# Attention and expert kernel on one core: attention-times-value groups merged in pairs, a ring of twelve exponentials, and row statistics written where they are used

## The chip, the cores and the metric

The kernel runs on one core of a Trainium2 chip. The metric is device microseconds of one execution, the median over runs. TensorE multiplies matrices and writes to the eight PSUM banks (512 fp32 columns each). VectorE, ScalarE and GpSimd do element work; SyncE and the others issue DMAs. Each engine takes its instructions in the order of its own program, and semaphores join the programs.

## The reference

Input x is 16 x 512 tokens of 256 features, so 8192 tokens. Then, cut to what matters:

```python
n = layernorm(x)
a = w[0] * mha(n @ proj_local, window=128) + w[1] * mha(n @ proj_global, window=256)
#   mha: 16 heads of 16; softmax(q @ k.T / 4 + mask) @ v; mask adds 1 above the diagonal
x1 = x + layernorm(layernorm(a) * gamma + beta)
y  = layernorm(x1)
moe = y + gate(token) * (silu(r @ w_gate[e]) * (r @ w_up[e])) @ w_down[e]
#   r = y's row; e = argmax of y @ w_router, 32 experts, at most 320 tokens of one expert, later ones dropped
out = x1 + layernorm(moe)
```

## The kernel before

**Two stages.** The attention stage goes over 32 windows of 256 tokens in a software pipeline of 36 steps. The expert stage then goes over 16 pairs of experts, from rows that the attention stage scattered to `slots_d` in HBM. In step s, window a = s is projected to q, k and v; b = s-1 has its row maxima found; c = s-2 has its exponentials and its value products; d = s-3 is projected out and normalised; f = s-4 is routed.

**Units and slots.** A window has 24 score units of 512 columns: 8 local ones (two heads of two 128-token blocks) and 16 global ones (one head). A step has 24 slots k. In each slot every engine does its part for unit k, and whatever the tables `PE_AT`, `ACT_AT` and `DVE_AT` put there: a name and the number of its slot. The order within a slot is that of the code of `step`.

- TensorE in slot k: `scores(k, c)` fills one of two banks `S2` with transposed scores (L1245, L1249 local; L1254, L1257 global), less each row's maximum, plus the mask. `tri` times the identity adds the mask. Then come the table's items, last `row_scores(k, b)` into one of two banks `S1` (L1316, L1319). Here `x2T` and `xnT` are transposes (L1351, L1357), `p0` to `p3` the q and k projections (L1288), `v0`, `v1` those of v (L1295), `lg` the router (L1371), `op0`, `op1` the output projection (L1398), `cs` the counts of the router (L1384 to L1388).
- ScalarE: `exps(k, c)` (L688) takes bank S2 to `pt`, a ring of 8 tiles of 128x512 fp32. Other items: `p` (high parts, L699), `mid` (L705), `v` (L711), and the scaling of normalised rows (L718): `norm0` the next x, `xn2` the router's input, `f1` and `z` the two inner layer norms.
- VectorE: `maximum(k, b)` (L922) reduces bank S1 to row maxima. Other items: `u` (below), `p` (L906), `f`, statistics (L849, L857), `top` and `route` (small router operations), `split` and `fold`.
- GpSimd: reciprocal roots of the variances (`inv_std`), low parts (L539), the scaling with gamma and beta, the sum `x1` (L587), and the scatter of rows (L576).

**Value products.** `values(g)` multiplies exponentials with `v_pad` for four heads into the one bank `PV`: heads go to 32-partition strips, so one matmul writes 32 partitions, and fp32 makes each matmul two instructions. A group fills 256 of the bank's 512 columns: four local groups of 16 instructions of 128 columns (L1270), four global ones of 16 of 256 columns (L1278). VectorE then turns PV in 32x32 blocks into `otok` (`unfold`, L949), after every second group takes the reciprocal of the softmax sums (L955) and multiplies (`normalise`, L963). The next `values` waits for `pv_read` of the last `unfold`. Groups 0 to 7 are at TensorE's slots 4, 6, 9, 12, 14, 18, 22 and 1 of the next step; unit u's exponential waits until the group that read its tile of the ring is through.

**Row statistics.** A token's row is 260 numbers in `xrow`: x1, mean, reciprocal deviation, gate, token number. VectorE copies mean and deviation (L1058, L1059), gate and token (L1028, L1029) into it and counts `left` down (L1035). The scatter writes the row out, and the expert stage normalises it as (x1 - mean) * rstd (L1130).

Of the kernel before, what the change touches and what calls it, by code (L numbers as in the profile page):

```python
# [8 lines left out]
def attention_moe_program(nc, T, x, pT_l, pT_g, winT_l, winT_g, woT_l, woT_g, bqk_l, bqk_g, bv_l, bv_g,  # L9
# [16 lines left out]
    GROUPS = 8  # L26
# [9 lines left out]
    MEAN, RSTD, GATE, TOKEN = D, D + 1, D + 2, D + 3  # L36
# [31 lines left out]
    with ExitStack() as ctx:  # L68
# [74 lines left out]
        okf = sb("okf", [P, 2])  # L143
        slotf = sb("slotf", [P, 2])
        far = sb("far", [P, 2])
        gate1 = sb("gate1", [P, 2])
# [3 lines left out]
        bvb = sb("bvb", [P, 4, P])  # L150
        bo = sb("bo", [P, 2, D])
# [200 lines left out]

        ACT_NORMS = (0, 1, 2, 3)
# [5 lines left out]
        def _(sp):  # L359
# [95 lines left out]
            sp.wait_ge(pv_full, GROUPS * NW)  # L455
# [25 lines left out]
        def _(pool):  # L481
# [28 lines left out]
            def inv_std(n, w):  # L510

                wait(pool, ln_var[n], w)
                if n in ACT_NORMS:
                    pool.tensor_tensor(nm[:, n, :], mv[:, n, :, 0], minus1[:, :], ALU.mult)  # L514
# [3 lines left out]
                if n in ACT_NORMS:  # L518
                    last.then_inc(rstd_made[n], 1)
                    wait(pool, rstd_made[n], w)  # L520
                    last = pool.tensor_tensor(mr[:, n, :], nm[:, n, :], rstd[:, n, :], ALU.mult)
                last.then_inc(ln_rstd[n], 1)

            def inv_std_again(w):

                wait(pool, rstd_made[3], w)
                pool.tensor_tensor(ve[:, 4, :], rstd[:, 3, :], rstd[:, 3, :], ALU.mult).then_inc(rstd_sq_made, 1)
# [14 lines left out]
            def step(s, par):  # L542
# [6 lines left out]
                if f:  # L549
                    inv_std(3, f)  # L550
                    inv_std_again(f)
# [27 lines left out]
                if d:  # L579
# [6 lines left out]
                    pool.wait_ge(xr_in[1 - par], xr_count(d))  # L586
                    pool.tensor_tensor(x1[:, 1 - par, :, :], ybuf[:, :, :], xr[:, 1 - par, :, :], ALU.add).then_inc(x1_ready, 1)  # L587
# [39 lines left out]
        def _(act):  # L627
# [51 lines left out]
            def exps(u, c):  # L679
                wait(act, s2_full, c, UNITS, u)  # L680

                if u < 8:
                    wait(act, pv_full, back(c), GROUPS, 6 + u // 4)
                elif u < 16:
                    wait(act, pv_full, c, GROUPS, (u - 8) // 2)
                else:
                    wait(act, pv_full, c, GROUPS, 4 + (u - 16) // 4)
                act.activation(pt[:, u % 8, :], S2[u % 2][:, :], ACT.Exp).then_inc(p_ready, 1)  # L688
# [18 lines left out]
            def v_out(q, b, par):  # L707
                wait(act, v_full, b, 2, q)

                wait(act, pv_full, back(b, 2), GROUPS, GROUPS - 1)  # L710
# [818 lines left out]
```

## Time and profile before

| | us |
|---|---|
| median of 3 runs (lowest, highest) | 1620.1 (1618.76, 1621.07) |
| profiled execution, its own time | 1606.68 |
| its span, first to last instruction | 1604.9 |
| mean granted TensorE clock | 0.973 |

The profiled execution is 13.4 us, 0.8%, below the median of the timed runs. The page has the busy time of every engine (PE is TensorE's matmuls, PEld its weight loads, DVE VectorE, ACT ScalarE, POOL GpSimd), and the chain that ended last. Rows of the timeline and of the chain are merged: "x16" is sixteen instructions of one line.

### The profile page before, as it was taken

Reading aid. Unit: us, or ns where it says so; the run is one execution under the profiler, and the core shown is the slowest. Engines: PE = TensorE matmul, PEld = TensorE weight load, DVE = VectorE, ACT = ScalarE, POOL = GpSimd, SP = SyncE. Lnnn points to the kernel's source line nnn. Section 1 sums busy time; section 2 is a strip of 40 time slices with the busy share of each in tenths; the row PEclk is TensorE's granted clock in tenths of the full one; section 3 lists DMA queues with packets and bytes.
Section 4 is the critical chain, followed back from the end, with each engine's and each line's share of the span. In section 5 each row is a group of like instructions: output and inputs, shape, how many; then the busy total and the mean of one; then the engine's idle time right before and its main releaser. Section 6 shows DMA issues by size and latency. Waiting matters only on the chain.

```text
span 1604.9 us, 39878 instructions
## 1 busy us (share of the span) xinstructions
PE 1496.9 (93%) x13672; PEld 1089.0 (68%) x13672; DVE 1240.0 (77%) x3785; ACT 912.3 (57%) x1919; POOL 725.1 (45%) x1097
## 2 busy tenths in 40 slices
PE   5799999999999999999999999999999945999992
PEld 3566777777777777777777777777777624777771
DVE  2677888888888888888888888888888632788874
ACT  3356667666666767666667676666666532222220
POOL 2113444444444444444444444444444341466666
PEclk9999999999999999999999999999999977999996
DMA  7997666666666766676666656656566303545540
GB/s 130 171 222 174 111 110 103 108 107 104 115 111 104 114 107 106 104 110 114 104 109 107 105 103 104 102 102 103 102 98 102 100 15 104 153 151 166 168 139 11
DMA packets 253720, 183.56 MB, mean 114 GB/s; under 512 B 29492, under 2 KB 252151, under 8 KB 253518
## 3 DMA queue, kind: packets, MB, share of 16 engines
q1 hardware_dynamic: 232414, 164.49, 55.7%
q10 hardware_dynamic: 14192, 12.79, 2.9%
q0 software_dynamic: 6912, 3.73, 0.9%
q8 instruction: 110, 1.80, 0.5%
q14 instruction: 92, 0.75, 0.2%
HBM read 55.78 MB, written 38.04 MB: 58 GB/s over the span
## 4 chain that ended last, share of the span: by engine, by line
PE 88%; DVE 2%; POOL 2%; issue 2%; DMA 2%; SPq 1%; ACT 1%; ACTq 1%; POOLq 0%; DVEq 0%
PE bank L1288 14%; PE bank L1439 9%; PE bank L1278 7%; PE bank L1319 7%; PE bank L1398 7%; PE bank L1295 7%; PE bank L1257 7%; PE bank L1270 4%; PE bank L1316 4%; PE bank L1254 3%; PE bank L1249 3%; PE bank L1245 3%; PE bank L1371 2%; PE bank L1452 2%; PE bank L1464 2%
## 5 line engine op out<-in xcount | busy, mean ns | idle before, releaser
L922 DVE TENSOR_REDUCE mx<-bank 128x2 f32<-128x512 f32 (+1 forms) x768 | 512.8, 672 | 154.8 <-PE bank L1316 96.2
L688 ACT ACTIVATE pt<-bank 128x512 f32<-128x512 f32 x768 | 449.7, 593 | 237.1 <-PE bank L1257 149.3
L1288 PE MATMUL bank<-xnT,weff 128*128 128x256 f32 x1024 | 253.8, 391 | 7.2 <-DVE rest L906 6.4
L1288 PEld LDWEIGHTS bank<-xnT,weff 128*128 128x128 f32 x1024 | 186.3, 192 | 42.1 <-issue 11.9
L1319 PE MATMUL bank<-stack 96*128 96x256 bf16 x1024 | 196.7, 273 | 5.9 <-DVE mx L922 5.7
L1257 PE MATMUL bank<-stack 100*128 100x128 bf16 x2048 | 197.9, 218 | 0.0
L539 POOL TENSOR_TENSOR parts<-rest,parts 128x512 bf16<-128x512 f32 x128 | 147.6, 1162 | 76.2 <-ACT parts L705 76.2
L554 POOL TENSOR_TENSOR obuf<-obuf,xrow 128x512 f32<-128x512 f32 x32 | 40.6, 1270 | 298.0 <-ACT obuf L730 298.0
L1257 PEld LDWEIGHTS bank<-stack 100*128 100x128 bf16 x2048 | 157.8, 97 | 12.6
L699 ACT ACTIVATE parts<-bank,bqk 128x256 bf16<-128x256 f32 x256 | 107.5, 471 | 101.7 <-PE bank L1288 99.2
L514 POOL TENSOR_TENSOR nm<-mv,minus 128x2 f32<-128x2 f32 x128 | 25.2, 197 | 273.0 <-DVE mv L857 269.9
L1439 PE MATMUL bank<-eT,ew 128*128 128x320 f32 x512 | 144.7, 436 | 0.6 <-ACT eT L808 0.6
L1319 PEld LDWEIGHTS bank<-stack 96*128 96x128 bf16 x1024 | 78.4, 98 | 97.4 <-issue 54.3
L1254 PE MATMUL bank<-tri,identb 128*128 128x256 bf16 x512 | 140.3, 274 | 3.2 <-ACT pt L688 2.5
L949 DVE STREAM_TRANSPOSE otok<-bank 128x256 f32<-128x256 f32 x256 | 112.4, 439 | 36.9 <-PE bank L1270 17.6
L1278 PE MATMUL bank<-pt,v_pad 128*32 128x256 f32 x2048 | 137.9, 387 | 2.5 <-ACT pt L688 1.3
L1398 PE MATMUL bank<-wo,OnT 128*128 128x256 f32 x512 | 128.2, 394 | 0.0
L1295 PE MATMUL bank<-weff,xnT 128*128 128x512 f32 x256 | 125.1, 611 | 0.9
L1439 PEld LDWEIGHTS bank<-eT,ew 128*128 128x128 f32 x512 | 96.9, 192 | 38.2 <-issue 2.4
L906 DVE SCALAR_TENSOR_TENSOR rest<-bank,bqk,parts 128x256 f32<-128x256 f32 x256 | 109.1, 467 | 14.9 <-ACT parts L699 14.9
L1316 PE MATMUL bank<-stack 96*128 96x128 bf16 x1024 | 100.1, 220 | 7.3 <-DMA stack<-parts 6.2
L1398 PEld LDWEIGHTS bank<-wo,OnT 128*128 128x128 f32 x512 | 93.9, 193 | 16.8 <-issue 6.2
(153 smaller groups left out, 2718.9 us busy)
## 6 DMA issues: line engine op xcount, KB each, us to landing
stack<-parts SPq DMA_DIRECT2D x768, 64.0 KB, 2.6
stack<-parts SPq DMA_DIRECT2D x378, 128.0 KB, 5.8
slots_scratch<-zeros ACTq DMA_DIRECT2D x16, 650.0 KB, 5.1
xr<-x SPq DMA_DIRECT2D x32, 256.0 KB
out<-obuf SPq DMA_DIRECT2D x32, 256.0 KB, 3.3
ew<-w_gate SPq DMA_DIRECT2D x32, 256.0 KB, 3.5
ew<-w_up SPq DMA_DIRECT2D x32, 256.0 KB, 5.0
ew<-w_down SPq DMA_DIRECT2D x32, 256.0 KB, 4.2
```

Source lines behind the costliest of these rows:

```text
L539: pool.tensor_tensor(parts[:, j, 2, :], rest[:, j % 2, :], parts[:, j, 1, :], ALU.subtract).then_inc(lo_ready, 1)
L688: act.activation(pt[:, u % 8, :], S2[u % 2][:, :], ACT.Exp).then_inc(p_ready, 1)
L922: dve.reduce_max(dst, src, AX.X).then_inc(s1_read, 1)
L1254: pe.matmul(diagonal, identb[:, :], tri[:, :].unsqueeze(1).to_broadcast([P, 2, P]), start=True, stop=False)
L1257: last = pe.matmul(bank[:, (2 * kb + qb) * P:(2 * kb + qb + 1) * P], k_stack(par, 1, u - LU, kb * P, P, BROW), q_stack(par, 1, u - LU, qb ...
L1278: last = pe.matmul(PV[32 * h4:32 * h4 + 32, 0:WIN], v_pad[:, par, kb, 1, 4 * (g - 4) + h4, :], pt[:, (u0 + h4) % 8, kb * WIN:(kb + 1) * WI ...
L1288: last = pe.matmul(bank[:, t * WIN:(t + 1) * WIN], weff[:, b, c, qk * D + t * P:qk * D + (t + 1) * P], xnT[:, par, c, :], start=(c == 0), ...
L1295: last = pe.matmul(pj_bank(f"v{q}")[:, :], xnT[:, par, c, q * P:(q + 1) * P], weff[:, :, c, 2 * D:3 * D], start=(c == 0), stop=(c == 1))
L1316: last = pe.matmul(bank[:, (2 * n + j) * P:(2 * n + j + 1) * P], q_stack(par, 0, 2 * u + n, j * P, P, NPART), k_stack(par, 0, 2 * u + n, j ...
L1319: last = pe.matmul(bank[:, n * WIN:(n + 1) * WIN], q_stack(par, 1, u - LU, n * P, P, NPART), k_stack(par, 1, u - LU, 0, WIN, NPART), start ...
L1398: last = pe.matmul(TR[:, q * D:(q + 1) * D], OnT[:, n // 2, n % 2, q * P:(q + 1) * P], wo[:, n, :], start=(n == 0), stop=(n == 3))
L1439: last = pe.matmul(banks[2 + 2 * m + n][:, 0:CAP], ew[:, e % 3, n, c, m * P:(m + 1) * P], eT[:, p % 2, c, e % 2 * CAP:(e % 2 + 1) * CAP], ...
```

## The change

- Groups 2g and 2g+1 become one: `values(g)` for g = 0 to 3 issues 32 matmul instructions into the whole bank, with one wait for the bank and one wait for exponentials (4g+3, then 15 and 23). `unfold` is one 512-column transpose. There are four where there were eight.
- The ring `pt` has 12 tiles. The groups stand at TensorE's slots 4, 12, 18 and 1; `unfold` at VectorE's 6, 13, 18 and 1.
- Global scores: two matmuls of 256 columns in place of four of 128, and the mask product comes last in place of first.
- `inv_std(3)` writes the deviation and the shift (-mean * rstd) straight into `xrow`; the scaling on ScalarE reads them there. The gate's reciprocal goes straight to `xrow`, GpSimd writes the token number, `far` comes from one operation. The expert stage computes x1 * rstd + shift.
- The three tables move other items, as the diff shows. Two set-up tiles share memory with `obuf` and `xn2`.

```diff
-    GROUPS = 8
+    PAIRS_PV = 4
+    PTR = 12
-            pt = sb("pt", [P, 8, 512], on=attn)
+            pt = sb("pt", [P, PTR, 512], on=attn)
-        PE_AT = {"xnT": 0, "g7": 1, "p0": 2, "x2T": 3, "mT_g": 4, "g0": 4, "p1": 5, "g1": 6, "lg": 6, "op0": 8, "op1": 9, "g2": 9,
-                 "p2": 11, "g3": 12, "cs": 13, "mT_l": 14, "p3": 14, "g4": 14, "v0": 17, "g5": 18, "v1": 20, "g6": 22}
-        ACT_AT = {"xnT": 0, "xn2": 1, "p0": 2, "mT_g": 4, "x2T": 4, "mid0": 5, "p1": 5, "o_norm": 7, "mid1": 8, "gate": 10, "p2": 11, "f1": 13, "mid2": 14, "mT_l": 14, "p3": 14, "mid3": 17, "v0": 17, "z": 21, "v1": 20, "norm0": 20}
-        DVE_AT = {"split_g": 0, "u7": 1, "p0": 3, "fold_g1": 4, "xn2": 3, "u0": 4, "p1": 6, "u1": 6, "top": 7, "u2": 9, "f": 9, "split_l": 10, "p2": 12, "u3": 12, "route": 14, "u4": 14, "fold_l0": 11, "p3": 15, "fold_l1": 14, "stats_x": 16, "stats_y": 17, "u5": 18, "fold_g0": 21, "u6": 22, "stats_x1": 23, "moments_x1": 0}
+        PE_AT = {"xnT": 0, "p0": 2, "x2T": 3, "mT_g": 4, "p1": 5, "lg": 7, "op0": 7, "op1": 9, "p2": 11, "cs": 14, "mT_l": 15, "p3": 15, "v0": 17, "v1": 20, "g3": 1, "g0": 4, "g1": 12, "g2": 18}
+        ACT_AT = {"xnT": 0, "xn2": 1, "p0": 2, "mT_g": 4, "x2T": 4, "mid0": 5, "p1": 5, "o_norm": 5, "mid1": 9, "gate": 10, "p2": 11, "f1": 14, "mid2": 14, "mT_l": 16, "p3": 15, "mid3": 17, "v0": 17, "z": 22, "v1": 20, "norm0": 18}
+        DVE_AT = {"split_g": 0, "p0": 3, "fold_g1": 4, "p1": 7, "top": 7, "f": 9, "split_l": 8, "p2": 12, "route": 14, "fold_l0": 10, "p3": 16, "fold_l1": 15, "stats_x": 16, "stats_y": 17, "fold_g0": 22, "stats_x1": 23, "moments_x1": 0, "u3": 1, "u0": 6, "u1": 13, "u2": 18}
...
-                last = pool.tensor_tensor(rstd[:, n, :], ve[:, n, :], mhalf[:, 0:2], ALU.pow)
+                scale, shift = (xrow[:, par, :, RSTD], xrow[:, par, :, SHIFT]) if n == 3 else (rstd[:, n, :], mr[:, n, :])
+                pool.tensor_tensor(scale, ve[:, n, :], mhalf[:, 0:2], ALU.pow).then_inc(rstd_made[n], 1)
...
                     pool.wait_ge(xr_in[1 - par], xr_count(d))
+                    pool.tensor_scalar(xrow[:, 1 - par, :, TOKEN], left[:, :], -float(WIN * num(d)), None, ALU.add)
                     pool.tensor_tensor(x1[:, 1 - par, :, :], ybuf[:, :, :], xr[:, 1 - par, :, :], ALU.add).then_inc(x1_ready, 1)
...
-                dve.transpose(otok[:, b, half, :], PV[:, 0:WIN]).then_inc(pv_read, 1)
+                dve.transpose(otok[:, b, :, :].rearrange("p s n -> p (s n)"), PV[:, :]).then_inc(pv_read, 1)
...
-                        dve.tensor_copy(xrow[:, par, :, MEAN], mv[:, 3, :, 0])
-                        dve.tensor_copy(xrow[:, par, :, RSTD], rstd[:, 3, :])
...
-                    pe.matmul(diagonal, identb[:, :], tri[:, :].unsqueeze(1).to_broadcast([P, 2, P]), start=True, stop=False)
                     for kb in range(2):
-                        for qb in range(2):
-                            last = pe.matmul(bank[:, (2 * kb + qb) * P:(2 * kb + qb + 1) * P],
-                                             k_stack(par, 1, u - LU, kb * P, P, BROW), q_stack(par, 1, u - LU, qb * P, P, BROW),
-                                             start=False, stop=(kb == 1 and qb == 1))
+                        pe.matmul(bank[:, kb * WIN:(kb + 1) * WIN], k_stack(par, 1, u - LU, kb * P, P, BROW),
+                                  q_stack(par, 1, u - LU, 0, WIN, BROW), start=(kb == 0), stop=False)
+                    last = pe.matmul(diagonal, identb[:, :], tri[:, :].unsqueeze(1).to_broadcast([P, 2, P]), start=False, stop=True)
...
                 else:
-                    u0 = LU + 4 * (g - 4)
-                    wait(pe, p_ready, c, UNITS, u0 + 3)
-                    for kb in range(2):
-                        for h4 in range(4):
+                    u0 = LU + 8 * (g - 2)
+                    wait(pe, p_ready, c, UNITS, u0 + 7)
+                    for half in range(2):
+                        for kb in range(2):
+                            for h4 in range(4):
```

## Rows read from the trace of the kernel before

**Rows 1.** The page: busy time, granted clock in 40 slices, the chain by engine.
```profile
PE 1496.9 (93%) x13672; PEld 1089.0 (68%) x13672; DVE 1240.0 (77%) x3785; ACT 912.3 (57%) x1919; POOL 725.1 (45%) x1097
...
PEclk9999999999999999999999999999999977999996
...
PE 88%; DVE 2%; POOL 2%; issue 2%; DMA 2%; SPq 1%; ACT 1%; ACTq 1%; POOLq 0%; DVEq 0%
```

**Rows 2.** TensorE's timeline, `p3` of two steps: start us, us, what.
```profile
599.70 1.99 PE L1288 MATMUL bank<-xnT,weff 128*128 128x256 f32 x8
...
638.30 1.99 PE L1288 MATMUL bank<-xnT,weff 128*128 128x256 f32 x8
```

**Rows 3.** Busy time of each engine over ten steps.
```profile
core 0: us, PE busy (x) PEld busy (x) DVE busy (x) ACT busy (x) POOL busy (x), PEclk, DMA share, GB/s
402.80:788.80 386.00, 385.69 (x3932) 282.71 (x3931) 324.86 (x1021) 266.14 (x560) 179.14 (x300) 1.00 0.64 107
```

**Rows 4.** The chain that ended last, 603 to 643 us: start us, its time.
```profile
603.90 1.98 PE bank L1295 x4
...
606.45 1.00 PE bank L1278 x16
607.45 0.33 PE bank L1319 x2
...
608.11 0.22 PE bank L1319 x2
608.33 0.11 PE bank L1254
608.44 0.23 PE bank L1257 x4
608.66 1.77 PE bank L1295 x4
...
616.76 1.78 PE bank L1288 x8
...
635.45 0.57 PE bank L1270 x16
636.03 0.32 PE bank L1319 x2
...
641.74 0.36 PE bank L1319 x2
```

**Rows 5.** The list of waits.
```profile
PEld bank L1295 <- DVE base L1015: 5.7, 28, 0.2
```

**Rows 6.** TensorE's timeline, units 20 to 23, then 0 and 1.
```profile
608.17 0.27 PE L1254 MATMUL bank<-tri,identb 128*128 128x256 bf16 x1
...
610.50 0.27 PE L1254 MATMUL bank<-tri,identb 128*128 128x256 bf16 x1
...
611.05 0.27 PE L1254 MATMUL bank<-tri,identb 128*128 128x256 bf16 x1
...
612.71 0.27 PE L1254 MATMUL bank<-tri,identb 128*128 128x256 bf16 x1
...
613.27 0.38 PE L1245 MATMUL bank<-tri,identb 128*128 128x512 bf16 x1
...
614.38 0.38 PE L1245 MATMUL bank<-tri,identb 128*128 128x512 bf16 x1
```

**Rows 7.** ScalarE's timeline over the same slots.
```profile
611.03 0.60 ACT L688 ACTIVATE pt<-bank 128x512 f32<-128x512 f32 x1
611.52 1.08 ACT L718 ACTIVATE ybuf<-ybuf,mr,rstd 128x256 f32<-128x256 f32 x2
612.51 0.58 ACT L688 ACTIVATE pt<-bank 128x512 f32<-128x512 f32 x1
...
616.77 1.09 ACT L718 ACTIVATE xn<-xrow,mr,rstd 128x256 f32<-128x256 f32 x2 [1.15 <-POOL mr L521]
```

**Rows 8.** Groups of instructions: busy us, mean ns, idle before.
```profile
L949 DVE STREAM_TRANSPOSE otok<-bank 128x256 f32<-128x256 f32 x256 | 112.4, 439 | 36.9 <-PE bank L1270 17.6 <-PE bank L1278 15.2
...
L1097 DVE TENSOR_TENSOR fbuf<-bank,bias_row 128x512 f32<-128x512 f32 x32 | 22.1, 692 | 33.0 <-PE bank L1398 33.0
L514 POOL TENSOR_TENSOR nm<-mv,minus 128x2 f32<-128x2 f32 x128 | 25.2, 197 | 273.0 <-DVE mv L857 269.9
...
L1058 DVE COPY xrow<-mv 128x2 f32<-128x2 f32 x32 | 5.1, 160 | 2.8 <-POOL mr L521 2.8
```

More of the change, by code:

```diff
@@ L719, in norm, with row_norm @@
                 last.then_inc(sem_, 1)
+            def row_norm(w, par):
+                wait(act, ln_rstd[3], w)
+                for q in range(2):
+                    last = act.activation(xn2[:, q, :], x1[:, par, q, :], ACT.Identity, bias=xrow[:, par, q, SHIFT:SHIFT + 1],
+                                          scale=xrow[:, par, q, RSTD:RSTD + 1])
+                last.then_inc(xn2_ready, 1)
             def first_norm(w, par):
@@ L760, in step @@
                         wait(act, x2T_full, back(f))
-                        norm(3, xn2, x1[:, par, :, :], xn2_ready, f)
+                        row_norm(f, par)
                     if f and k == ACT_AT["x2T"]:
@@ L1065, in step @@
                             route_top(part, f)
-                    if d and k == DVE_AT["u7"] + 1:
-                        sums(7, d)
-                    if d and k == DVE_AT["u7"] + 2:
-                        normalise(7, d)
+                    if d and k == DVE_AT["u3"] + 1:
+                        sums(3, d)
+                    if d and k == DVE_AT["u3"] + 2:
+                        normalise(3, d)
                     if d and k == DVE_AT["fold_g1"]:
                         fold(1, 1, d)
-                    for g in (1, 3, 5):
+                    for g in range(PAIRS_PV - 1):
                         if c and k == DVE_AT[f"u{g}"] + 1:
@@ L1076, in step @@
                             normalise(g, c)
-                    for g in range(GROUPS - 1):
+                    for g in range(PAIRS_PV - 1):
                         if c and k == DVE_AT[f"u{g}"]:
                             unfold(g, c)
-                    if d and k == DVE_AT["u7"]:
-                        unfold(7, d)
+                    if d and k == DVE_AT["u3"]:
+                        unfold(3, d)
                     for chunk in range(2):
@@ L1089, in step @@
                             rest_part(j, a)
-                    for part in range(6):
+                    for part in range(5):
                         if f and k == DVE_AT["route"] + part:
@@ new lines, in values @@
+                wait(pe, pv_read, c if g else back(c), PAIRS_PV, (g - 1) % PAIRS_PV)
+                if g < 2:
+                    wait(pe, p_ready, c, UNITS, 4 * g + 3)
+                    for half in range(2):
+                        for j in range(2):
+                            for h4 in range(4):
+                                u = 4 * g + 2 * half + h4 // 2
+                                last = pe.matmul(PV[32 * h4:32 * h4 + 32, half * WIN + j * P:half * WIN + (j + 1) * P],
+                                                 v_pad[:, par, j, 0, 8 * g + 4 * half + h4, :],
+                                                 pt[:, u % PTR, (2 * (h4 % 2) + j) * P:(2 * (h4 % 2) + j + 1) * P],
+                                                 start=True, stop=True)
+                else:
+                    u0 = LU + 8 * (g - 2)
+                    wait(pe, p_ready, c, UNITS, u0 + 7)
+                    for half in range(2):
+                        for kb in range(2):
+                            for h4 in range(4):
+                                last = pe.matmul(PV[32 * h4:32 * h4 + 32, half * WIN:(half + 1) * WIN],
+                                                 v_pad[:, par, kb, 1, 8 * (g - 2) + 4 * half + h4, :],
+                                                 pt[:, (u0 + 4 * half + h4) % PTR, kb * WIN:(kb + 1) * WIN], start=(kb == 0), stop=(kb == 1))
@@ L1358, in step @@
                         last.then_inc(xnT_full, 1)
-                    for g in range(GROUPS - 1):
+                    for g in range(PAIRS_PV - 1):
                         if c and k == PE_AT[f"g{g}"]:
                             values(g, c, par)
-                    if d and k == PE_AT["g7"]:
-                        values(GROUPS - 1, d, 1 - par)
+                    if d and k == PE_AT["g3"]:
+                        values(PAIRS_PV - 1, d, 1 - par)
                     if c and k == PE_AT["mT_g"]:
```

94 lines of the change are left out of this document (32 added, 62 removed).

## The prediction

> **What bounds the kernel now.** I read four views. The page first: TensorE is busy 93% of the span, and 88% of the chain that ended last is TensorE's, where no other engine has more than 2% [rows 1]. Then the timeline, for the period: the same projection starts at 599.70 and 638.30, so a full step takes 38.60 us [rows 2], and ten steps in a row show TensorE busy for 385.69 of 386.00 us, at full clock, with VectorE at 324.86, ScalarE at 266.14 and GpSimd at 179.14 [rows 3]. So the attention stage is TensorE's queue and hardly anything else. A saved TensorE time is saved 32 times; a saved VectorE time is worth nothing, unless TensorE was waiting for it. VectorE, however, is busy 84% and has only two banks of slack, and ScalarE has the same two-bank slack for the exponentials. Third, the chain in detail shows what a block of value products costs, and how much TensorE waits. Fourth, ScalarE's timeline, since the tables move its work. The expert stage is untouched but for one operation of the same form.
>
> **Value products, the gain.** A projection's instruction of 256 columns takes 1.78 / 8 = 0.2225 us in the chain [rows 4]. In a value block four strips run side by side, so 16 instructions are four such passes: 0.89 us if nothing else were paid. The block takes 1.00, and the two row-score matmuls behind it take 0.33 where they take 0.22 elsewhere [rows 4]: 0.11 on the way in, 0.11 on the way out, together 0.22. A local block has half the columns: 0.445 against 0.57, and 0.32 against 0.22 behind it [rows 4]: 0.225. Merging two blocks pays this once in place of twice. 32 windows x 4 pairs x 0.223 = 28.6 us. The column passes themselves stay. That is the upper bound. The lower: only the 0.11 behind a block is saved, and the second half of a merged block starts as slowly as a block does: 128 x 0.11 = 14.1 us. I take the upper, because inside a block the passes already follow each other at the plain rate, and the second half is the same pattern in other columns.
>
> The Trainium skill, TensorEngine Tiling (Array Packing), § Key Properties, says that changing the tiling mode drains TensorE, while changing only the tile does not. The trace agrees with a price at both ends of a block, 0.11 and 0.11 us [rows 4]. By that rule a merged block has two changes of mode where two blocks had four, so the gain would be 28.6 us; if the entry price were no drain but the start of each half, 14.1 us.
>
> **Global scores.** Four matmuls of 128 columns take 0.23, two of 256 (the row scores) take 0.22, and the mask product takes 0.11 in either order [rows 4]. 0.00 to 0.01 x 512 units = 0 to 5 us. Both figures are rounded, and at full clock the columns are what is paid, so I take 0. What ends a unit is now the mask product, at the same distance from its start.
>
> **VectorE, hidden.** It loses four transposes of 0.439 a step and gains 512 columns in each of the others. No row shows a 512-column transpose. From below it costs as much as 256 columns, 0.44; from above twice that, 0.88. Another fp32 read of 512 columns from PSUM takes 0.692 [rows 8]; I take 0.70, so 8 x 0.439 - 4 x 0.70 = 0.71 us less a step. The copies into the row go (four of about 0.16 [rows 8]), and two more small operations. Together some 1.5 us less of VectorE's 32.5 a step. What covers it is that TensorE is the bound; the cover is gone only where TensorE waits for VectorE, which is the next part. At its dearest, 0.88, VectorE still has less to do than before.
>
> For that transpose, the Trainium skill, VectorE: DVE Perf Modes, § The TRN2 errata, states 120 + FD cycles for a read from PSUM at 0.96 GHz: 0.66 us for 512 columns (its 0.39 for 256 is below the 0.439 measured here). The sum is the same by either.
>
> **TensorE's waits before.** `v0` takes 1.98, `v1` 1.77 [rows 4]: 0.21 lost each step, where `v0`'s bank is still read by VectorE's `base` (28 waits are listed at the weight loads [rows 5]). One pair of row scores takes 0.36 in place of 0.22 [rows 4], behind a late maximum: 0.14. Together 0.35 a step. After the change VectorE has 1.5 us less, but merged work stands in larger lumps: before `base` are now a 0.70 transpose in slot 13, a `normalise` and a `fold` in slot 15, and TensorE's filler between slots 12 and 17 is one value block shorter. Between 0 and 0.5 for both; I take 0.30, so 0.05 is gained.
>
> **ScalarE at the end of a step, the loss.** This is the place that the tables make worse. Take the start of unit 20 (608.17) as zero; the starts after it are 2.33 (unit 21), 2.88 (22), then before the change a value block, 4.54 (23), 5.10 (unit 0 of the next window), 6.21 (unit 1) [rows 6]. Without the block of slot 22, 1.10 us go: unit 23 starts at 3.44, unit 0 at 4.00, unit 1 at 5.11. ScalarE's exponential 21 starts 0.53 after its unit (611.03 against 610.50), the next instruction 0.49 after that, and `z`, two instructions, takes 0.99 to the next start (611.52 to 612.51) [rows 6, 7]. `z` moves from slot 21 to 22. So: exponential 22 at 2.88 + 0.53 = 3.41, `z` at 3.90, exponential 23 at 4.89, done 0.58 later at 5.47. Unit 1 writes the bank that exponential 23 reads, so it starts at 5.53, 0.42 late. Behind it in TensorE's queue are the merged group 3, `p0` and all else. From both sides: 0 if ScalarE were ahead by more, 0.6 if `z` also waited for its variance. I take 0.42.
>
> **The router's row scaling and group 0.** The chain `z`, sum x1, statistics, root, `xn2` runs from 611.52 to the end of `xn2` at 617.86 [rows 7]: 6.34 us. GpSimd now also writes the token number ahead of x1, about 0.2 (its 128x2 operations take 0.197 [rows 8]). So `xn2` ends at 3.90 + 6.34 + 0.2 = 10.44 on the clock above. Behind it on ScalarE are exponential 2, the high parts of `p0` and exponential 3: about 0.5 + 0.8 + 0.6, done at 12.3. Group 0 in slot 4 waited for unit 1 before; now it waits for unit 3. TensorE comes to it at 5.53 + 0.44 (unit 1) + 2.00 (group 3) + 0.22 + 0.44 + 1.78 (`p0`) + 0.22 + 0.44 + 0.44 (`x2T`) + 0.22 + 0.44 = 12.2. So 0.1 late; 0 to 0.3.
>
> **The ends.** In the last window nothing covers group 3: a block of 2.0 in place of 1.0, and 0.26 more of transpose, less some 0.3 of small operations in the last routing chain: +1 us, 0 to 2. The clock is below full around the change of stages (the two sevens [rows 1]), because TensorE idles there; a shift of a microsecond may move when it rises again, by some us in either direction.
>
> **Sum.** -28.6 for the blocks. Per full step +0.42 + 0.10 - 0.05 = +0.47; I count 29 such steps, but the loss overlaps in part with what VectorE would cost in the same slots, so 0.40 x 29 = +11.6. Ends +1. Total -16.0 us. Against the profiled execution's own 1606.7 that is 1590.7; the profile lies 13.4 below the median of the runs, so I carry the difference: 1620.1 - 16.0 = 1604.1, call it 1604.
>
> **Rivals.** *No new wait:* ScalarE and VectorE keep up, the whole 28.6 stays: 1592. For it: every term of the loss rests on margins of half a microsecond, and VectorE has less to do. Against it: `z` in slot 22 with the filler of that slot gone. *The halves pay as before:* only 14.1 is gained and the 11.6 lost: 1619, no change that can be told; this is the case in which the merge does not do what it says. For it: nothing in the trace shows a block of 32. Against it: the passes inside a block. *Slower:* group 0's wait. It hangs on a chain through four engines whose slack I put at -0.1 us; each further 0.1 costs 0.1 a step. From 0.65 us on, the kernel is slower than before by more than can be put down to chance; at 1.0 us it is 1604 + 29 = 1633. For it: ScalarE already sits idle 1.15 us before `xn2`, waiting for GpSimd [rows 7]. Against it: the chain's pieces keep their sizes, and its start moves with TensorE.
>
> **How the numbers follow.** Forecast 0.52 (own range 1596 to 1612), no new wait 0.26, halves 0.12, slower 0.10. A range of 1588 to 1617 leaves out the slower case and the tails: 8 in 10. Faster by over 0.2% (below 1616.9): the first two, 0.78. Within 0.2%, about what a measurement of this kernel can tell from none: 0.12. Slower: 0.10.
>
> **What the profile after would show.** A merged global block of about 1.89 us and a local one of 1.00, each with 0.33 behind it, would show the gain; 2.0 and 1.14 would show that halves pay. The period of a full step should be about 38.60 - 0.89 + 0.40 = 38.1 us. A wait of unit 1's mask product for ScalarE of about 0.4 us, once a step, would show the loss; `v0` near 1.9. The transpose should show near 0.70. If TensorE waits before group 0 by more than 0.3, or the period is above 38.6, the prediction is wrong, and the last rival is the first suspect.

## The result and the profile after

Four timed runs of the changed kernel have a median of 1573.96 us (1571.47 to 1580.65), four of the kernel before one of 1619.43. The ratio is 0.9725 [0.9705, 0.9744]. The forecast was 1604 (1588 to 1617): right in sign, but a gain of 16 us where 45 were measured, and the time lies outside the range.

The profiled execution took 1575.8 us, its span is 1574.1. The page of the changed kernel, busy times, clock and chain, answers to [rows 1]:

```profile
PE 1460.0 (93%) x12648; PEld 1065.3 (68%) x12648; DVE 1195.8 (76%) x3465; ACT 905.1 (58%) x1919; POOL 736.4 (47%) x1129
...
PEclk9899999999999999999999999999999967999996
...
PE 79%; issue 5%; SPq 4%; POOL 3%; ACT 3%; DMA 3%; DVE 2%; ACTq 1%; POOLq 0%; DVEq 0%
```

TensorE is still busy 93%, with 37 us less to do. Its timeline, `p3` of two steps, answers to [rows 2], and a stretch of ten steps to [rows 3]:

```profile
811.95 1.89 PE L1275 MATMUL bank<-xnT,weff 128*128 128x256 f32 x8
...
849.22 1.89 PE L1275 MATMUL bank<-xnT,weff 128*128 128x256 f32 x8
```

```profile
402.80:775.53 372.73, 371.52 (x3611) 274.32 (x3610) 310.14 (x920) 263.34 (x560) 183.03 (x310) 1.00 0.67 110
```

A full step takes 37.27 us where it took 38.60. Most steps take just that; the mean of the last 27 is 37.34. The chain after, start and time, answers to [rows 4]:

```profile
587.69 1.73 PE bank L1275 x8
...
593.12 1.86 PE bank L1264 x32
594.99 0.32 PE bank L1306 x2
595.31 0.22 PE bank L1239 x2
595.53 0.11 PE bank L1241
...
596.19 1.72 PE bank L1282 x4
...
598.50 0.02 ACT pt L680
...
599.54 0.78 ACT ybuf L710 x2
...
600.53 0.59 ACT pt L680
```

The merged global block takes 1.86 and has 0.32 behind it, as the upper estimate had it. `v0` and `v1` take 1.72, less than any such group before. At the turn of the step the chain goes through ScalarE, through `z` (L710) and an exponential (L680). TensorE's share of the chain fell from 88% to 79%; ScalarE's rose from 1% to 3%, those of issue and of SyncE's queue rose by 3 points each. A page's group for the transpose:

```profile
L947 DVE STREAM_TRANSPOSE otok<-bank 128x512 f32<-128x512 f32 x128 | 90.7, 709 | 15.7 <-PE bank L1264 12.5 <-PE bank L1254 3.0
```

0.709 us where 0.70 was taken. Start to start, as means over the full steps of both traces, TensorE's full step comes apart like this:

| us per step | forecast | measured |
|---|---|---|
| value blocks, their entries and exits | -0.89 | -0.95 |
| waits of before (a row score 0.15, ahead of `v0` 0.20, small 0.03) | -0.05 | -0.38 |
| fp32 groups `lg`, `op`, `p2`, `p3`, `v0`, `v1` | 0 | -0.44 |
| global scores themselves, 16 units | 0 | -0.08 |
| turn of the step, unit 21 to unit 1 | +0.42 | +0.49 |
| group 0's wait; `cs` | +0.10; 0 | +0.01; +0.05 |
| sum | -0.42 | -1.30 |

The mean period fell by 1.26 (by 1.33 in a step that nothing disturbs); the 0.04 to the sum is spread in pieces of a few ns. The row of the fp32 groups has two causes. `p2`, `v1`, `op1`, `p3` and `v0` each lose 0.055, 0.28 in all, which the runs below tie to the order of the global scores. Besides, `lg`, `op1` and `p3` lose 0.05 each because they no longer stand behind a value block, `v0` loses as much because it no longer waits, and `op0`, now behind `lg`, takes 0.03 more.

From the fourth `p3` to the last, 27 steps, the changed kernel takes 34.0 us less. It comes to the fourth 2.4 us later and takes 0.7 longer behind the last, which makes the 30.8 between the spans, to a rounding. The 2.4 belong to this execution: the fourth `p3` starts at 177.5 us here and at 175.1 before, but at 169.9 and 173.0 in two later profiles of the changed kernel. The other 15 us of the 45 are in neither trace; the runs on the chips below are about them.

The kernel before took 1619 to 1621 us in three sets of runs and 1605 to 1606 in three others; each set of the experiments ran on a chip of its own. Ratios below are to the runs of before in the same set.

### The profile page after: what moved, and what is told of

Its sections match the earlier page's. It is cut to its first block, busy times and chain, and to the rows that moved or that the text cites. A ratio compares the mean times of both kernels' runs of the same rounds, so it can differ in the third digit from the quotient of the medians.

```text
span 1574.1 us, 37380 instructions
## 1 busy us (share of the span) xinstructions
PE 1460.0 (93%) x12648; PEld 1065.3 (68%) x12648; DVE 1195.8 (76%) x3465; ACT 905.1 (58%) x1919; POOL 736.4 (47%) x1129
## 4 chain that ended last, share of the span: by engine, by line
PE 79%; issue 5%; SPq 4%; POOL 3%; ACT 3%; DMA 3%; DVE 2%; ACTq 1%; POOLq 0%; DVEq 0%
PE bank L1275 13%; PE bank L1426 9%; PE bank L1264 7%; PE bank L1385 7%; PE bank L1282 6%; PE bank L1306 6%; PE bank L1239 5%; PE bank L1254 4%; PE bank L1303 3%; PE bank L1229 3%; PE bank L1233 3%; PE bank L1241 3%; PE bank L1358 2%; PE bank L1439 2%; PE bank L1451 2%
## 5 line engine op out<-in xcount | busy, mean ns | idle before, releaser
L680 ACT ACTIVATE pt<-bank 128x512 f32<-128x512 f32 x768 | 444.4, 592 | 189.3 <-PE bank L1241 154.0
L1239 PE MATMUL bank<-stack 100*128 100x256 bf16 x1024 | 196.5, 273 | 3.3 <-ACT pt L680 2.5
L1306 PEld LDWEIGHTS bank<-stack 96*128 96x128 bf16 x1024 | 84.3, 98 | 96.1 <-DVE mx L921 38.8
L1264 PE MATMUL bank<-pt,v_pad 128*32 128x256 f32 x2048 | 125.1, 385 | 1.6 <-ACT pt L680 1.6
L1385 PE MATMUL bank<-wo,OnT 128*128 128x256 f32 x512 | 124.7, 387 | 0.0
L1282 PE MATMUL bank<-weff,xnT 128*128 128x512 f32 x256 | 120.4, 593 | 1.1 <-DVE base L1013 1.1
L1239 PEld LDWEIGHTS bank<-stack 100*128 100x128 bf16 x1024 | 95.0, 97 | 22.0 <-ACT pt L680 4.8
L1229 PE MATMUL bank<-tri,identb 128*128 128x512 bf16 x256 | 97.8, 382 | 11.1 <-ACT pt L680 5.1
L947 DVE STREAM_TRANSPOSE otok<-bank 128x512 f32<-128x512 f32 x128 | 90.7, 709 | 15.7 <-PE bank L1264 12.5
```

What stands on the lines that cost most here:

```text
L680: act.activation(pt[:, u % PTR, :], S2[u % 2][:, :], ACT.Exp).then_inc(p_ready, 1)
L1239: pe.matmul(bank[:, kb * WIN:(kb + 1) * WIN], k_stack(par, 1, u - LU, kb * P, P, BROW), q_stack(par, 1, u - LU, 0, WIN, BROW), start=(kb = ...
L1264: last = pe.matmul(PV[32 * h4:32 * h4 + 32, half * WIN:(half + 1) * WIN], v_pad[:, par, kb, 1, 8 * (g - 2) + 4 * half + h4, :], pt[:, (u0 ...
L1282: last = pe.matmul(pj_bank(f"v{q}")[:, :], xnT[:, par, c, q * P:(q + 1) * P], weff[:, :, c, 2 * D:3 * D], start=(c == 0), stop=(c == 1))
L1306: last = pe.matmul(bank[:, n * WIN:(n + 1) * WIN], q_stack(par, 1, u - LU, n * P, P, NPART), k_stack(par, 1, u - LU, 0, WIN, NPART), start ...
L1385: last = pe.matmul(TR[:, q * D:(q + 1) * D], OnT[:, n // 2, n % 2, q * P:(q + 1) * P], wo[:, n, :], start=(n == 0), stop=(n == 3))
```

## The experiments

### Global scores alone, and in the old form

*The two new 256-column products with the mask last, in the kernel before* (in the changed one the edit is the reverse):

```diff
-                    pe.matmul(diagonal, identb[:, :], tri..., start=True, stop=False)
                     for kb in range(2):
-                        for qb in range(2):
-                            last = pe.matmul(bank[...128 columns...], ...)
+                        pe.matmul(bank[:, kb * WIN:(kb + 1) * WIN], ..., start=(kb == 0), stop=False)
+                    last = pe.matmul(diagonal, identb[:, :], tri..., start=False, stop=True)
```

> The kernel before with one part of the change alone: global scores as two matmuls of 256 columns, the mask product last. Theory A (the first fp32 weight load behind a 128-column bf16 matmul is exposed by 0.055 us, behind a 256-column one it is hidden): v0, v1, p2 and op1, which stand right behind such a unit, each lose 0.055 from 1.77 to 1.78 us; value blocks still pay their entry; with 16 x 0.003 for the wider matmuls the step falls from 38.60 to about 38.3, the time by 8 to 12 us. Theory B (the prediction's: order and width are worth nothing): step 38.55 to 38.60, time within 3 us of before.

1616.79 us, ratio 0.9963 [0.9949, 0.9977]. That is 5 to 6 us, less than the 8 to 12 expected: `op0`, `p2` and `v1` got 0.055 shorter, while `v0` still waits for `base`, and `op1` and `p3` stand behind a value block there and keep their 1.83 and 1.92.

*Only the mask product moved to the end, still four products of 128 columns.*

> The kernel before with the mask product of the global scores last, but still four matmuls of 128 columns. Theory A: the whole of the saving at the fp32 groups comes from the last matmul being 256 columns wide, so this run has the same 0.055 at v0, v1, p2 and op1 as the run with both; only 0.05 us a step of the wider matmuls is missing, step about 38.35. Rival (it is the number of matmuls and weight loads that pays): nothing here, step 38.6.

1616.12 us, ratio 0.9965 [0.9953, 0.9977]. So it is the place of the mask product, not the number of matmuls. The chain of this run shows what it does:

```profile
608.72 0.11 PE bank L1259
608.83 1.72 PE bank L1295 x4
...
617.26 0.23 PE bank L1249 x4
617.49 1.78 PE bank L1288 x8
...
633.67 0.11 PE bank L1259
633.78 1.73 PE bank L1288 x8
```

L1259 is the mask product (256 columns), L1249 the local scores (128 columns each). An fp32 group behind the first takes 1.72 or 1.73, behind the second 1.78: 0.055 us less, in whichever line it is. The likeliest reading is that the weight load of the group's first instruction hides behind 256 columns and not behind 128; the trace shows the times, not the reason.

*The changed kernel with the mask first and four products.*

> The kernel after with the global scores of before (mask product first, four matmuls of 128 columns). Theory A: the step rises from 37.27 by about 0.3 to 37.55, the time by 8 to 10 us. Theory B: no change, 37.27 to 37.30.

1598.75 us, ratio 0.9851 [0.983, 0.9872]; before took 1621.45 there. Against the changed kernel's 0.971 to 0.9725 that is 20 to 23 us lost, in a step that takes 38.07 on average. Five groups at 0.055 make 0.28 of it. The first full step of this trace takes 37.56, just what theory A says. In the 26 others, 37.89 to 38.37, TensorE also waits longer at the turn of the step, and there ScalarE stands idle for exponential 22:

```profile
609.31 0.60 ACT L680 ACTIVATE pt<-bank 128x512 f32<-128x512 f32 x1 [0.50 <-PE bank L1241]
```

Its unit had ended at 608.57, 0.74 earlier; usually the exponential follows by 0.20. `z`, exponential 23 and the scores behind them are late by as much. So the scores' own order is worth 0.3 a step, 8 us. The other 12 to 15 come with a late signal, which the changed kernel's own trace has in one step; the section on the chips returns to it. No run of this version was made on a chip where before takes 1605 us.

*The local units' mask product last too, in the changed kernel.*

```diff
-                    pe.matmul(bank[:, :], identb[:, :], tri..., start=True, stop=False)
...
-                            last = pe.matmul(..., start=False, stop=(h2 == 1 and j == 1))
+                            pe.matmul(..., start=(h2 == 0 and j == 0), stop=False)
+                    last = pe.matmul(bank[:, :], identb[:, :], tri..., start=False, stop=True)
```

> The changed kernel with the mask product of the local units last too (it was only the global units' that moved). Theory A (a fp32 group whose first weight load follows a wide bf16 product is 0.055 us shorter than behind a 128-column one, and the mask product of a local unit is 512 columns wide): xnT, p0, x2T, p1 and lg, five groups in each step, give 5 x 0.055 = 0.28 us per step, 8 us in all, ratio to the changed kernel 0.995. Theory B (the groups behind local units wait for their data or for row scores, so nothing is given back): the same time within 2 us.

1571.28 us, ratio to before 0.9681 [0.9664, 0.9697]; the changed kernel on that chip 0.971 [0.9696, 0.9724]. `p0`, `p1` and `lg` took 0.058 less each, `xnT` and `x2T` 0.01 or less: 0.17 to 0.19 of the 0.28, and some 0.04 came back as waits. The gain is 3.5 us by the medians and 4.6 by the ratios, where 8 were expected. A chain row of it:

```profile
608.91 0.22 PE bank L1234
609.12 1.73 PE bank L1275 x8
```

### The merge

*The changed kernel, each block of 32 split into two of 16 with the slot's row scores between.*

```diff
+                        values(g, c, par, 0)     # half 0 ahead of the row scores
...
+                        values(g, c, par, 1)     # half 1 behind them, then pv_full
```

> The kernel after with each value block issued in two halves of 16 instructions, the row scores of the unit between them; same bank, same transposes, same waits. If what the merge saves is the entry and the exit of a block (0.09 + 0.02 and 0.12 us), the step rises by four times 0.23, from 37.3 to 38.2, and the time by 25 to 30 us. If entering costs nothing and only leaving is paid, half of that. If the gain came from fewer waits and signals, nothing.

1602.11 us where before took 1604.78, ratio 0.9978 [0.996, 0.9997]; the changed kernel took 1571.9 on a chip of that kind (below). That is 30 us between runs on two chips, where 128 x 0.223 = 28.5 was the price; the step is 38.17 in place of 37.27. The chain shows it:

```profile
593.08 0.57 PE bank L1254 x16
593.66 0.32 PE bank L1307 x2
593.98 0.57 PE bank L1254 x16
594.56 0.32 PE bank L1239 x2
```

Each half pays 0.57 and has 0.32 behind it; whole, the local block takes 1.01 to 1.05 and has one 0.32 behind it. The merge pays per block, and all of it. The ring of 12 and the one wait for exponentials stand in this run as in the changed kernel, so they are not what it measures; no run tries the ring by itself.

### ScalarE at the turn of the step

*`z` at 21, where it was, and at 23.*

```diff
-"z": 22   (ACT_AT)
+"z": 21   and, in the other run, "z": 23
```

> The kernel after with the scaling z on ScalarE back in slot 21, one number in the table. If z between the exponentials 22 and 23 is what makes TensorE late at the end of a step (0.43 us a step beside an undisturbed one: 0.26 at unit 1, the rest at units 22 to 0), most of it goes: step about 36.9 to 37.0, time 8 to 12 us less. Rival: ScalarE's exponentials are late by their number alone in four slots without filler, and z one slot earlier only moves the wait to unit 23: less than 0.15 a step.

1589.66 us, ratio 0.9813 [0.9791, 0.9834].

> The kernel after with the scaling z on ScalarE in slot 23, one later than after and two later than the run that was 1% slower. If z ahead of an exponential is what makes TensorE late (exponential 22 in that run, 23 in the kernel after), z behind exponential 23 delays only exponential 0, which has the 1.9 us of value block 3 to spare: the wait at unit 1 of 0.26 us goes, step 37.0 to 37.1, time 5 to 8 us less. Rival: the sum x1 and all behind it start 0.5 us later, and group 0 waits for exponential 3 by as much: no gain.

1593.98 us, ratio 0.9928 [0.9908, 0.9947]. Both are slower than with 22. In either the wait ahead of unit 1 is gone (0.26), as the theory said, and another takes its place: at 21 exponential 22 stands behind `z` and unit 0 waits 0.97, 0.86 more than in the changed kernel; at 23 the chain behind `z` is late and `x2T` waits for `xn2` in nearly every step, the second row being group 0's:

```profile
PE bank L1338 <- ACT xn L716: 31.4, 27, 16.0
PE bank L1254 <- ACT pt L680: 10.8, 28, 0.4
```

Against unit 20 `z` starts 0.65 later than in the changed kernel, and TensorE comes 0.26 sooner; `x2T` is 0.36 late. So `xn2`'s chain had about 0.5 us of slack, and group 0's wait, which I had made a rival, is there with 0.46 as soon as `z` moves.

*The faster version: statistics of x and y a slot earlier, `f1` at 13, `z` at 19, local mask last.*

```diff
-"f1": 14, "z": 22 (ACT_AT); "stats_x": 16, "stats_y": 17 (DVE_AT)
+"f1": 13, "z": 19 (ACT_AT); "stats_x": 15, "stats_y": 16 (DVE_AT)
```

> A version meant to be faster than the changed kernel: the local units' mask product last as well, and ScalarE's row at the turn of the step eased. VectorE's statistics of the next x move from slot 16 to 15 and those of y from 17 to 16, ScalarE's f1 from 14 to 13, z from 22 to 19. Theory A (norm0 waits 2.1 us for GpSimd and pushes v1's copy, four exponentials and z into one stretch, so units 0 and 1 wait 0.31 us): norm0 starts 2 us earlier, z is done before unit 20, the waits ahead of units 0, 1, 22 and 23 fall by 0.3 to 0.43 us per step; with the 0.15 us of the mask product 13 to 16 us under the changed kernel, 1558 to 1562 us. Theory B (VectorE, 76% busy, becomes late in slots 14 to 17 and row scores there wait): what ScalarE gives is taken back, within 4 us of the changed kernel. A third way: z at slot 19 waits for GpSimd as it did at 21 and blocks exponential 20: 10 us over the changed kernel.

1562.49 us (1556.77 to 1565.77), ratio 0.9712 [0.9695, 0.973]; the changed kernel on the same chip 1571.92, 0.9789 [0.9773, 0.9805]. It is 9 us faster than the changed kernel by the medians and 12 by the ratios, less than the 13 to 16 expected; the full steps of its trace, 37.12 against 37.30, give 5 of them. Unit 1's wait went (0.26), the mask brought 0.17, but exponential 21 is now behind `v1`'s copy and unit 23 waits 0.30:

```profile
PEld bank L1239 <- ACT pt L680: 15.7, 31, 1.5
```

*The same with `v1`'s copy one slot later.*

> The version with z at 19 and the statistics a slot earlier, which took 1562 us, with ScalarE's copy of v1 moved from slot 20 to 21, behind exponential 21. Theory A (there unit 23's scores wait 0.30 us for exponential 21, which stands behind the copy of 0.48 us): the wait goes, 0.30 us in each of 28 steps, 8 us less, 1553 to 1556 us. Theory B (the mask rows that a DMA brings to unit 0, or VectorE's maxima at units 22 and 23, end last right behind it): under 2 us, 1560 to 1563 us.

1568.65 us, ratio 0.9774 [0.9752, 0.9797]. The 0.30 went, and 0.45 appeared ahead of unit 0, since the copy now stands ahead of exponential 22. Three moves, and each time ScalarE's one extra piece of 0.5 to 1.0 us only passed from one unit to another.

*GpSimd's scatters moved out of the way of x1.*

```diff
-                if f: (two indirect_dma_start)          # ahead of x1
+                if exists(back(s, 5)): (the same two)   # next step, behind inv_std_again
```

> The changed kernel with GpSimd's two indirect scatters moved from ahead of the residual sum x1 into the next step, behind the row statistics, where GpSimd waits 5 us for nothing. Theory A (the two scatters, 2.4 us, make x1 start 0.4 us behind the end of z, and the normalised rows and the exponential behind them late by as much): x1 starts 0.4 us earlier and the waits at the turn of the step shrink by 0.1 to 0.2 us, 3 to 6 us in all. Theory B (the waits at the turn come from z ahead of exponential 23 alone, and what follows x1 has slack): the same time within 2 us. A third way: the scatters now lie beside the first value groups of a step and slow something there, up to 5 us more.

1577.61 us, ratio 0.9717 [0.9694, 0.974]; the changed kernel beside it 1574.73 (ratio 0.971). No gain. GpSimd, idle for 3.09 us, now waits for `z` ahead of the token number, and x1 starts only 0.1 sooner behind it: x1 had waited for `z`, not for the scatters. The third way came too, in small: the transposes of maxima behind group 0 take 0.34 where they took 0.22, and most steps are 37.41.

### The waits of before, and VectorE

*The kernel before with the row statistics in place, and nothing else of the change.*

> The kernel before with one part of the change alone: row statistics and gate written in place, token number by GpSimd, one operation less for far, slot numbers one slot earlier. VectorE has 0.87 us less a step. If the waits of TensorE for VectorE before the change (0.42 us a step in slots 15 to 17) went by this part, the time falls by 8 to 13 us. If they went with the value blocks and the tables, this is within 4 us of before: VectorE is ahead of these waits by its order, not by its load.

1608.38 us, ratio 1.0013 [1.0, 1.0026]; the step 38.60 as before, with the same waits. VectorE's busy time fell by 0.38 a step (321.10 against 324.86 us in ten steps), less than the 0.87 that I had counted. What it saved is worth nothing there.

*The kernel before with group 3's product a slot earlier.*

```diff
-                        if c and k == DVE_AT[f"u{g}"] + 2:
+                        if c and k == DVE_AT[f"u{g}"] + (1 if g == 3 else 2):
                             normalise(g, c)
```

> The kernel before with one VectorE instruction moved: the product of the outputs by the reciprocals of group 3 stands one slot earlier (slot 13 in place of 14). In the trace of before this product takes 1.23 us where the three others of a step take about 0.4, and lies under GpSimd's scaling by gamma. Theory A (the two share something, the 0.8 us that VectorE loses makes the base sum of the routing and with it v0 late): the mean of that group falls from 601 to about 420 ns, the waits ahead of v0 of 0.25 us per step go, 7 us in all (ratio 0.9955), and the remaining 0.145 us ahead of p3 stays, since p3 there stands right behind a value block. Theory B (v0 waits for something else): the same time as before within 2 us, whatever the product takes.

1621.63 us, ratio 1.0009 [0.9995, 1.0022]. Two groups, the first of before, the second of this run:

```profile
L963 DVE TENSOR_TENSOR On<-otok,rden 128x256 f32<-128x256 f32 x128 | 77.0, 601 | 0.0
```

```profile
L963 DVE TENSOR_TENSOR On<-otok,rden 128x256 f32<-128x256 f32 x128 | 54.1, 422 | 1.1
```

And from this run's list of waits:

```profile
PEld bank L1295 <- DVE base L1015: 5.8, 28, 0.2
```

The product no longer lies under GpSimd's and takes 0.42; `v0` waits as before. Theory A fell. In this trace VectorE, done early, waits 0.72 for TensorE's next scores, and then does `p3`'s rest ahead of the base sum all the same. The 0.15 is, by the timeline, no wait of `p3`, as I had written: it stands ahead of a row score in three slots without filler, where TensorE makes a unit each 0.56 us and a maximum takes 0.6 to 0.65.

*The kernel before with `p3`'s rest a slot later, as the changed kernel has it.*

```diff
-"p3": 15   (DVE_AT)
+"p3": 16
```

> The kernel before with VectorE's rest of projection 3 moved one slot back, from 15 to 16, where the changed kernel has it, behind the base sum of the routing. Theory A (v0 waited for the base sum because this rest of 0.87 us stood ahead of it; the product that lies under GpSimd's work was ruled out by the run before): the wait ahead of v0 of 0.2 us goes, the wait for L1015 in the list of waits is gone, 6 to 7 us off the time of before (ratio 0.996). Theory B (the place is taken by another wait, v1's or that of a row score behind the moved rest): within 2 us of before.

1606.36 us, ratio 1.0012 [1.0001, 1.0023]. `v0`'s wait is gone from the list, 0.24 a step; 0.29 came two units later. The chain there:

```profile
604.06 0.86 DVE rest L906 x2
...
606.44 0.66 DVE bst L849 x2
607.10 0.09 DVE mv L857 x2
607.19 0.64 DVE mx L922
607.83 0.05 issue
607.88 0.39 PE bank L1319 x2
```

A row score waits for a maximum behind a queue of VectorE's work, 5 us of it in a row, from 602.75 to 607.83 in this chain. But the move did more than reorder. With the rest gone, a small product (`posh`) came to lie beside GpSimd's low parts (602.30 to 603.45), and grew from 270 to 675 ns in the mean. First before's group, then this run's:

```profile
L1016 DVE TENSOR_TENSOR posh<-pos,hot 128x64 f32<-128x64 f32 x32 | 8.6, 270 | 0.0
```

```profile
L1016 DVE TENSOR_TENSOR posh<-pos,hot 128x64 f32<-128x64 f32 x32 | 21.6, 675 | 0.0
```

That 0.41 a step went into the very stretch whose end is late. So this run does not tell a wait that only moves from a wait that this product made.

### Two kinds of chip

*The kernel before once more.*

> The kernel before, unchanged, profiled a second time. The first profile (1606.7 us, step 38.60 in every step) lies 13 us below the timed runs, and the variants with the new scores, whose TensorE work is 0.5 us a step shorter, show steps of 38.9 and times of 1617. Theory C: the first profile caught an unusual execution; the usual one loses some 0.4 us more in each step, at the turn of the step, and this profile shows steps of 38.9 to 39.1 and a wait ahead of unit 0's row scores. Rival: the step is 38.60 again, and the 13 us lie outside the full steps.

1605.7 us, beside 1604.78 for before in the same set, step 38.60: the profile shown ahead of the prediction was no accident, it is what such a chip does.

*The changed kernel again, on two chips.* On one where before took 1621.14: 1574.73, ratio 0.971 [0.9696, 0.9724]. On the other:

> The changed kernel once more, to have it beside variants of before on one chip. Theory A (the kernel before loses 13 to 16 us on some chips to the late signal ahead of its transpose in slot 22, the changed kernel has no block there and loses nothing): 1572 to 1577 us on any chip, a ratio of 0.971 where before takes 1620 us and 0.981 where it takes 1605 us. Theory B (chips differ in something that both kernels feel): a ratio of 0.971 on any chip, 1559 us where before takes 1605 us.

1571.92 where before took 1605.3, ratio 0.9789 [0.9773, 0.9805]. The changed kernel takes nearly the same on both; it is before that differs, by 16 us.

The three traces of variants of before from the 1620 us chips (new scores, mask last, product moved) have one thing that the others lack. VectorE's timeline, the transpose of group 6 at the turn of a step, first of before, then of the run with the product moved:

```profile
612.62 0.45 DVE L949 STREAM_TRANSPOSE otok<-bank 128x256 f32<-128x256 f32 x1 [0.31 <-PE bank L1278]
```

```profile
619.26 0.45 DVE L949 STREAM_TRANSPOSE otok<-bank 128x256 f32<-128x256 f32 x1 [1.15 <-PE bank L1278]
```

The second run's list of waits has a row that before has not:

```profile
PE bank L1316 <- DVE mx L922: 9.6, 30, 0.6
```

The block's matmuls had begun 1.14 us earlier in the first and 1.98 in the second (617.28): the same release comes 0.84 later, two maxima behind it are late, and unit 0's row scores wait, 30 times in that trace; the step is 39.08 where it was 38.60. 27 steps give 13 of the 16 us. The changed kernel has no block in slot 22.

It is not the transpose's signal alone. In the same place ScalarE, idle, gets TensorE's signal for exponential 23 late as well, 0.74 behind the start of the unit's four last products (618.63) where before has 0.42 (612.83). Again first before, then the run with the product moved:

```profile
613.25 1.26 ACT L688 ACTIVATE pt<-bank 128x512 f32<-128x512 f32 x2 [0.16 <-PE bank L1257]
```

```profile
619.37 1.08 ACT L688 ACTIVATE pt<-bank 128x512 f32<-128x512 f32 x2 [0.40 <-PE bank L1257]
```

In the six traces of before and its variants that take 1605 us, no exponential for which ScalarE stood idle follows its unit by more than 0.20 us. On the 1620 us chips it happens once in nearly every step in these three traces, in the changed kernel with the old scores, and in the one with the scatters moved. The last is telling: there the late signal stands at the new place of the scatters, between the two, and no longer at the turn.

```profile
609.48 1.10 POOL L534 DMA_INDIRECT slots_scratch<-xrow,slot_u  x1 [0.18 <-issue]
...
611.57 0.60 ACT L684 ACTIVATE pt<-bank 128x512 f32<-128x512 f32 x1 [0.84 <-PE bank L1237]
```

By these traces a signal of TensorE on such a chip that falls near GpSimd's scatters can come some half a microsecond late. The unmoved changed kernel meets this in only 4 steps of its trace from such a chip.

*The transpose one slot later, twice.*

> The kernel before with VectorE's transpose of value group 6 moved one slot back, from 22 to 23 (TensorE makes the group in slot 22 as before). In three profiles of variants of before, of spans 1613 to 1621 us, this transpose starts 0.8 us after its block's matmuls have ended, the maxima of units 22 and 23 stand behind it and row scores of unit 0 wait 0.5 us in nearly every step; in the two profiles with spans of 1605 and 1606 us it starts at once and nothing waits. Theory A (that signal is late on some chips, and this is the 16 us between the two times of the kernel before): where before takes 1620 us, the move takes 10 to 14 us off; where before takes 1605 us, nothing. Theory B (the difference between the chips lies elsewhere): the same time as before on either, within 2 us.

1606.44 us, ratio 1.0011 [0.9999, 1.0022], on a chip where before takes 1605.3; and again 1606.76, ratio 1.0003 [0.9988, 1.0019], where before takes 1606.33. Both chips were of the kind on which nothing is to be gained, so the theory was not put to its test. That the late signals follow the scatters rests on one run; why only some chips have them stays open.

## Why the prediction was wrong

- *Value blocks:* right. -0.89 forecast, -0.95 measured; that halves might pay as before was a rival, and the split kernel refuted it with 30 us.
- *Transpose 0.70:* 0.709, right. *VectorE's load worth nothing:* right in the kernel before, by the run that lightened it alone.
- *Global scores, priced at 0 with bounds 0 to 5:* this step failed. I compared the times of the unit's own three matmuls and not of what follows. Every fp32 group right behind a global unit got 0.055 shorter, three groups in before and five in the changed kernel, and the units 0.08 a step. By itself that was worth 5 to 6 us in before. In the changed kernel it is 8 us of work, and 20 to 23 us on a chip with late signals. No row of before has an fp32 group behind 256 columns, so the 0.055 could not be read there; but a bound for it was missing. The other 0.16 of the fp32 row is the tables' doing, which the forecast put at nothing as well.
- *TensorE's waits before, 0.30 of 0.35 kept:* this step failed too. All 0.38 went. I had tied them to two instructions; the traces show a stretch of VectorE's queue that ends late, and none of three single edits brought time. The new tables put `p3` between slots that had no filler, leave one transpose, in slot 13, where there were two, in 12 and 14, and bring the product of group 3 out from under GpSimd's work (its group's mean is 420 ns, not 601). That these together end the waits is argued from the two traces, not shown: no run made only these moves.
- *The turn of the step, +0.42:* 0.49, right in size, and in part in its place. Of it 0.26 is the forecast wait of unit 1 for exponential 23; another 0.11 stands ahead of unit 0, and some 0.11 around the row scores of three slots without filler, where VectorE's maxima are slower than TensorE's units. `z` at 21 or 23 was worse still, so it was the best place for it in that table, and not the fault it looked like.
- *Group 0's wait, +0.10:* 0.01, within its bounds.
- *Outside the full steps:* the forecast comes to -2.7 there (blocks of five more windows -4.5, the loss in two more steps +0.8, the ends +1); it was +3.1, of which 2.4 are the first steps of this execution.
- *From profile to median:* the forecast carried 13.4 us of difference as if it belonged to every kernel. This step failed as well. It belonged to the kernel before on some chips, a further 13 to 16 us of the gain. A profile and timed runs that disagree by more than five times the spread of the runs should have widened the range. So should the forecast's own bounds: with 28.6 for the blocks, 5 for the scores and 0.35 in 29 steps for the waits, and no loss, its sum is 1576, and neither a rival nor the range went below 1588.

Of the 30 us missed, 15 are the last point's. The other 15 are the two failed steps, 0.33 + 0.44 + 0.08 in 27 steps or 23 us, less 2 for the small terms in these steps and 6 for what lies outside them.

## What to carry to other kernels

Price an edit of a queue by what stands behind it as well: a reordering at no cost took 0.055 us off each of five groups that it did not touch. A wait that names one instruction may be the visible end of a full stretch: count the stretch's work. When an instruction is moved to test a wait, compare the mean time of every instruction around it, since one that comes to lie beside another engine's work can grow and undo the test. And when the profiled execution lies outside the timed runs, the difference may belong to this kernel on some chips alone; it is no constant to carry over.

## What the runs showed of the hardware

- An fp32 group of eight matmuls of 256 columns or four of 512 took 1.77 or 1.78 behind a bf16 product of 128 columns, 1.72 or 1.73 behind one of 256; behind one of 512, eight of 256 took 1.73.
- A product of two SBUF operands on VectorE took 1.23 us in place of 0.42 when GpSimd's product with gamma lay beside it, once a step; moved ahead of it, VectorE's took 0.42. A product of 64 columns went from 0.27 to 0.68 beside GpSimd's low parts. Before's timeline:

```profile
600.10 1.23 DVE L963 TENSOR_TENSOR On<-otok,rden 128x256 f32<-128x256 f32 x1
```

- The kernel before took 1605 us on some chips and 1621 on others, while the changed kernel took 1572 to 1575 on either kind. On the slower ones some of TensorE's signals reached VectorE and ScalarE 0.2 to 0.8 us late near GpSimd's scatters.
